# The turned edge order of a graph attention layer, worked out beside another layer's gathers

## The reference, cut to what matters

```python
def _L2_gnn_ref(x, edge_index, W, b):
    ...
    norm = dinv[src] * dinv[dst]
    xw = x @ W
    msgs = xw[src] * norm[:, None]
    agg = jax.ops.segment_sum(msgs, dst, num_segments=n)
    return jax.nn.relu(agg + b)

def _L3_gnn_ref(triplet_h, src, dst, Wqkv, bqkv, ...):
    h = layernorm(triplet_h, ln_attn_g, ln_attn_b)
    qkv = (h @ Wqkv + bqkv).reshape(n, 3, H, DH)
    ...
    scores = jnp.einsum('ehd,ehd->eh', q[src], k[dst])
    m = jax.ops.segment_max(scores, dst, num_segments=n)
    e = jnp.exp(scores - m[dst])
    sa = e / jax.ops.segment_sum(e, dst, num_segments=n)[dst]
    agg = jax.ops.segment_sum((v[src] * sa[:, :, None]).reshape(-1, D), dst, num_segments=n)
    ...
```

## Time and profile before

| | |
|---|---|
| median of 3 runs | 6839.76 us (6832.01 to 6848.44) |
| the profiled execution | 6829.43 us, span 6827.7 us |
| busy in the span | PE 45%, DVE 56%, ACT 26%, POOL 47% |
| DMA | 1056.28 MB, mean 155 GB/s |
| mean granted clock of TensorE | 0.713 of full speed |

### The profile page before, as it was taken

One profiled execution on the slowest core, in us unless ns is written; L12 is line 12 of the kernel. 1 busy time (PEld: TensorE's weight loads), 2 busy tenths in 40 slices (PEclk: granted clock), 3 DMA queues, 4 the chain that ended last, 5 costly groups with the idle time before them and its releaser, 6 DMA issues. The chain is left out here.

```text
span 6827.7 us, 78796 instructions
## 1 busy us (share of the span) xinstructions
PE 3084.9 (45%) x12973; PEld 1829.8 (27%) x12999; DVE 3813.8 (56%) x9383; ACT 1758.2 (26%) x4531; POOL 3197.0 (47%) x3216
## 2 busy tenths in 40 slices
PE   4467100345566666796001795001100157777638
PEld 3333100232243333343000342000100045555415
DVE  8998555467757776544334544344533546565551
ACT  1166000022226663111332211332100013232211
POOL 0000477667747773002776003776377625444430
PEclk9999555655567887898555897555555578888869
DMA  0000355456635553233665333665266428777630
GB/s 3 0 0 27 134 198 193 156 175 203 208 124 188 189 186 104 93 153 127 209 210 186 113 152 134 209 209 170 97 209 210 164 93 281 264 254 263 217 61 19
DMA packets 376599, 1056.28 MB, mean 155 GB/s; under 512 B 73682, under 2 KB 161140, under 8 KB 329876
## 3 DMA queue, kind: packets, MB, share of 16 engines
q1 hardware_dynamic: 211780, 588.53, 22.9%
q0 software_dynamic: 164688, 466.32, 22.6%
HBM read 537.47 MB, written 517.10 MB: 154 GB/s over the span
## 5 line engine op out<-in xcount | busy, mean ns | idle before, releaser
L940 POOL DMA_INDIRECT rows<-typed_table,index x832 | 813.1, 977 | 1183.1 <-DVE index L964 930.3
L940 POOL DMA_INDIRECT out_of<-table,index x936 | 968.4, 1035 | 464.9 <-issue 283.5
L979 DVE SCALAR_TENSOR_TENSOR state<-state,by_target_keep,rows 128x256 f32<-128x256 f32 x1248 | 604.8, 485 | 948.6 <-ACT rows L958 543.4
L940 POOL DMA_INDIRECT rows<-table,index x728 | 727.5, 999 | 317.8 <-issue 221.4
L1109 PE MATMUL bank<-ident,tail 128*128 128x128 f32 x6 | 2.0, 434 | 1658.8 <-PEq L74 1658.8
L2211 PE MATMUL bank<-weights,out_of 128*128 128x512 f32 x1600 | 698.3, 595 | 26.8 <-DVE weights L2259 26.8
L2603 POOL DMA_INDIRECT qv<-qv_table,index x416 | 410.6, 987 | 405.7 <-DVE index L2780 287.1
L979 DVE SCALAR_TENSOR_TENSOR y<-y,by_source_anew,out_of 128x256 f32<-128x256 f32 x897 | 435.4, 485 | 292.1 <-DMA out_of<-table,index 193.6
L958 ACT ACTIVATE rows<-rows,by_target_weight 128x256 f32<-128x256 f32 x832 | 343.0, 494 | 754.5 <-DMA rows<-typed_table,index 754.5
L1739 PE MATMUL bank<-x,marks 128*128 128x416 f16 x1664 | 392.8, 408 | 222.3 <-ACT marks L1753 222.3
L1109 PEld LDWEIGHTS bank<-ident,tail 128*128 128x128 f32 x6 | 0.9, 204 | 1659.9 <-issue 1659.9
(11 more groups left out here) (502 smaller groups left out, 6611.2 us busy)
## 6 DMA issues: line engine op xcount, KB each, us to landing
states<-state SPq DMA_DIRECT2D x195, 1024.0 KB, 4.3
states<-y SPq DMA_DIRECT2D x117, 1024.0 KB, 4.5
typed_table<-staged SPq DMA_DIRECT2D x400, 256.0 KB, 2.0
wide_states<-y SPq DMA_DIRECT2D x52, 1088.0 KB
near<-k_rows SPq DMA_DIRECT2D x416, 128.0 KB
out_of<-table,index POOLq DMA_INDIRECT x936, 2.9
rows<-typed_table,index POOLq DMA_INDIRECT x832, 2.9
rows<-table,index POOLq DMA_INDIRECT x728, 2.9
```

Of the source, the lines that this page charges most:

```text
L940: pool.indirect_dma_start(out=rows[h][:, u * D:(u + 1) * D], out_offset=None, in_=table, in_offset=bass.IndirectOffsetOnAxis(ap=index[h][: ...
L979: nc.vector.scalar_tensor_tensor(out=state[h][:, u * D:(u + 1) * D], in0=before, scalar=marks[:, bass.ds(g * GROUP + u, 1)], in1=rows[h][: ...
```

## The change

`StepOrder` becomes a companion. Its object is made at the start of the program, and `normalised_layer` hands it to the gather pass as `beside`, with `y` as the `spare` buffer. The phase of its own is gone. The DMAs are issued by ScalarE in place of SP; TensorE's part and VectorE's instructions are the same, VectorE's under `ahead`. `group` and `behind` are empty. Its ten semaphores are now among those of the pass (`step` and `cut` bear other names in the list).

```diff
-def normalised_layer(nc, env, order, x, out, own, w_dram, bias_dram, table, states):
+def normalised_layer(nc, env, order, x, out, own, w_dram, bias_dram, table, states, spare, steps):
...
-        edge_pass(nc, env, order, table, states, "sum", tail, [(bias[:], spread(bias_dram))], prepare=finish.prepare)
+        edge_pass(nc, env, order, table, states, "sum", tail, [(bias[:], spread(bias_dram))], prepare=finish.prepare, spare=spare, beside=steps)
...
 class StepOrder:
 
-    def __init__(self, stack, nc, by_source, by_target):
+    late = True
+    names = ("ready", "filed", "loaded0", "loaded1", "turned", "made", "marked", "summed", "settled", "kept")
+
+    def __init__(self, stack, nc, env, by_source, by_target, flat, window_table, k_rows):
...
-    def fill(self, nc, env, order, flat, window_table, k_rows):
...
-                @block.sync
-                def _(sp):
-                    sp.dma_start(flats[0].rearrange("(p t) -> p t", t=STEPS), order.keep[:]).then_inc(filed, 16)
...
+    def room(self, stack):
...
+        self.source_f, self.inner, self.total, self.quiet = (sb(n, STEPS) for n in ("source_f", "inner", "total", "quiet"))
...
+    def share(self, block, sems):
...
+        @block.scalar
+        def _(act):
+            nc.scalar.dma_start(flats[0].rearrange("(p t) -> p t", t=STEPS), order.keep[:]).then_inc(filed, 16)
+            act.wait_ge(ready, 1)
+            nc.scalar.dma_start(flats[1].rearrange("(p t) -> p t", t=STEPS), source_f[:]).then_inc(filed, 16)
+            act.wait_ge(filed, 32)
+            for a in range(2):
+                nc.scalar.dma_start(bulk(rows[a][:, 0:whole], MANY), flats[a][0:whole * P].rearrange("(k r q) -> r k q", k=MANY, r=P)
+                             ).then_inc(loaded[a], 16)
+                nc.scalar.dma_start(rows[a][0:rest, whole:whole + P], flats[a][whole * P:SLOTS].rearrange("(r q) -> r q", q=P)
+                             ).then_inc(loaded[a], 16)
+            act.wait_ge(ready, 2)
+            nc.scalar.dma_start(k_rows[ROWS:WINDOW_ROWS, :], zero[:]).then_inc(kept, 16)
+            act.wait_ge(settled, 1)
+            nc.scalar.dma_start(window_table.rearrange("u o -> o u"), self.window[0:1, :]).then_inc(kept, 16)
+            act.wait_ge(kept, 32)
...
+    def group(self, dve, g, h):
+        pass
+
+    def behind(self, dve):
+        pass
+
+    def ahead(self, dve):
...
+        then = counted_steps(dve, step)
+        nc.vector.tensor_copy(source_f[:], order.source[:]).then_inc(ready, 1)
+        nc.vector.memset(zero[:], 0.0).then_inc(ready, 1)
...
+        dve.wait_ge(turned, 1)
+        nc.vector.tensor_scalar(out=self.first[:], in0=env.bank[0][:, 0:STEPS], scalar1=-1.0, scalar2=1.0,
+                                op0=ALU.mult, op1=ALU.add).then_inc(cut, 1)
...
-            steps.fill(nc, env, order, flat, window_table, k_rows)
             row_norm(nc, x, y, gain[:], shift[:])
...
+        steps = StepOrder(stack, nc, env, by_source, by_target, flat, window_table, k_rows)
         x, y = buffer(stack, nc, "x", TILES * D), buffer(stack, nc, "y", TILES * D)
```

More of the change, by code:

```diff
@@ L2322 @@
 class StepOrder:
-    def __init__(self, stack, nc, by_source, by_target):
+    late = True
+    names = ("ready", "filed", "loaded0", "loaded1", "turned", "made", "marked", "summed", "settled", "kept")
+    def __init__(self, stack, nc, env, by_source, by_target, flat, window_table, k_rows):
+        self.nc, self.env, self.order = nc, env, by_target
+        self.flat, self.window_table, self.k_rows = flat, window_table, k_rows
         def sb(what, cols, dt=FP32):
@@ L2331, in __init__ @@
         self.place, self.chain_row = sb("place", TILES, I32), sb("chain_row", TILES, I32)
-    def fill(self, nc, env, order, flat, window_table, k_rows):
[L2336 to L2348, removed]
-                @block.sync
-                def _(sp):
-                    sp.dma_start(flats[0].rearrange("(p t) -> p t", t=STEPS), order.keep[:]).then_inc(filed, 16)
[L2353 to L2413, removed]
-                    then(nc.vector.tensor_tensor_scan(out=base[:], data0=env.ones[:, 0:TILES], data1=env.bank[7][:, 0:TILES], initial=0.0,
-                                                      op0=ALU.mult, op1=ALU.add))
-                    then(nc.vector.tensor_scalar(out=node[:], in0=env.iota_a1[:], scalar1=-1.0, scalar2=float(P), op0=ALU.add, op1=ALU.mult))
-                    then(nc.vector.tensor_scalar(out=node[:], in0=node[:], scalar1=env.own[:, 0:1], scalar2=base[:, TILES - 1:TILES],
-                                                 op0=ALU.add, op1=ALU.add))
-                    then(nc.vector.tensor_tensor(out=base[:], in0=base[:], in1=env.bank[7][:, 0:TILES], op=ALU.subtract))
-                    then(nc.vector.tensor_tensor(out=self.compact[:], in0=base[:], in1=env.bank[6][:, 0:TILES], op=ALU.add))
-                    then(nc.vector.tensor_tensor(out=node[:], in0=node[:], in1=self.compact[:], op=ALU.subtract))
-                    then(nc.vector.tensor_tensor(out=base[:], in0=self.compact[:], in1=node[:], op=ALU.subtract))
-                    then(nc.vector.tensor_tensor(out=base[:], in0=base[:], in1=order.some[:], op=ALU.mult))
-                    then(nc.vector.tensor_tensor(out=self.place[:], in0=base[:], in1=node[:], op=ALU.add))
-                    def step_of(out, edge):
-                        then(nc.vector.tensor_scalar(out=out[:], in0=edge[:], scalar1=0.5, scalar2=1.0 / P, op0=ALU.add, op1=ALU.mult))
-                        then(nc.vector.tensor_scalar(out=out[:], in0=out[:], scalar1=-0.5, scalar2=ROUND, op0=ALU.add, op1=ALU.add))
-                        then(nc.vector.tensor_scalar(out=out[:], in0=out[:], scalar1=-ROUND, scalar2=None, op0=ALU.add))
-                    step_of(base, order.start)
-                    then(nc.vector.tensor_copy(self.step_in[:], base[:]))
-                    then(nc.vector.tensor_tensor(out=last[:], in0=order.start[:], in1=order.count[:], op=ALU.add))
-                    then(nc.vector.tensor_scalar(out=last[:], in0=last[:], scalar1=-1.0, scalar2=0.0, op0=ALU.add, op1=ALU.max))
-                    step_of(step_out, last)
-                    then(nc.vector.tensor_tensor(out=last[:], in0=step_out[:], in1=base[:], op=ALU.is_gt))
-                    then(nc.vector.tensor_tensor(out=last[:], in0=last[:], in1=order.some[:], op=ALU.mult))
-                    then(nc.vector.scalar_tensor_tensor(out=step_out[:], in0=step_out[:], scalar=-float(STEPS), in1=last[:], op0=ALU.add, op1=ALU.mult))
-                    then(nc.vector.tensor_scalar(out=self.chain_row[:], in0=step_out[:], scalar1=float(STEPS), scalar2=None, op0=ALU.add))
-                    dve.wait_ge(summed, 2)
-                    then(nc.vector.tensor_copy(self.local[:], env.bank[2][:, 0:STEPS]))
-                    then(nc.vector.tensor_scalar(out=self.back_mark[:], in0=env.bank[5][:, 0:STEPS], scalar1=NEG, scalar2=None, op0=ALU.mult))
-                    then(nc.vector.memset(self.first[0:1, :], 1.0))
@@ new lines, in room, with sb @@
+    def room(self, stack):
+        def sb(name, cols, dt=FP32):
+            return buffer(stack, self.nc, name, cols, dt)
+        self.source_f, self.inner, self.total, self.quiet = (sb(n, STEPS) for n in ("source_f", "inner", "total", "quiet"))
+        self.rows = [sb("rows", (MANY + 1) * P) for _ in range(2)]
+        self.shifted, self.zero = sb("shifted", P + 1), sb("zero", D)
+        self.base, self.of_node, self.last, self.step_out = (sb(n, TILES) for n in ("base", "of_node", "last", "step_out"))
@@ new lines, in share, with _ @@
+    def share(self, block, sems):
+        nc, env, order = self.nc, self.env, self.order
+        self.sems = sems
+        ready, filed, loaded0, loaded1, turned, step, cut, summed, settled, kept = sems
+        loaded, rows, whole, rest = (loaded0, loaded1), self.rows, MANY * P, STEPS - MANY * P
+        inner, shifted, source_f, zero, k_rows, window_table = self.inner, self.shifted, self.source_f, self.zero, self.k_rows, self.window_table
+        flats = [self.flat[a * SLOTS:(a + 1) * SLOTS, :].rearrange("s o -> (s o)") for a in range(2)]
+        @block.scalar
[14 more added lines that the diff above has]
+            act.wait_ge(kept, 32)
+        @block.tensor
+        def _(pe):
+            for a in range(2):
+                pe.wait_ge(loaded[a], 32)
+                for k in range(MANY):
+                    nc.tensor.transpose(env.bank[a][:, k * P:(k + 1) * P], rows[a][:, k * P:(k + 1) * P], env.ident[:])
+                nc.tensor.transpose(env.bank[a][:, whole:STEPS], rows[a][0:rest, whole:whole + P], env.ident[0:rest, 0:rest]).then_inc(turned, 1)
+            pe.wait_ge(cut, 1)
+            nc.tensor.matmul(env.bank[3][:, 0:STEPS], env.ones[:], self.first[:], start=True, stop=True)
+            nc.tensor.matmul(env.bank[4][:, 0:STEPS], env.ones[0:1, :], self.first[0:1, :], start=True, stop=True)
```

(18 more changed lines are left out.)

52 lines of the change are left out of this document (added).

## The result

The changed kernel takes 6814.71 us (median of 9 runs, 6799.0 to 6828.71) against 6844.69 us before (9 runs, 6832.01 to 6848.44): ratio 0.9959, 95% interval 0.9947 to 0.9971. The forecast was 0.35% and 6816 us. Timed again in five rounds it was 0.9969 (0.9957 to 0.998). The medians are 30.0 us apart the first time and 24.1 the second, and the two profiled spans 6827.7 - 6803.0 = 24.7 us; so these measures of the gain lie between 24 and 30 us.

A forecast was written before the change was run, and what follows sets the result against it. No engine was busy over 56% of the span; POOL's gather chain was taken to set the pass's end. Terms -26.5 + 2.0 + 0.6 = -23.9 us, from 6839.8 to 6815.9 us (0.35% faster), range 6804 to 6833.

The forecast's parts named there:

- The sum: Whole kernel: -26.5 removed + 2.0 for slowed gathers + 0.6 for semaphores = -23.9 us.
- Removed, 26.5 us: Phase working out the turned edge order, between two barriers: cutting it saves 5507.83 - 5481.30 = 26.5 us.
- The ring covers the companion: Gather pass, third batch-normed layer: four loaded groups hide the companion's 25.0 us before fold group 0; cost nothing.
- my 5.6: Cover left in us: fifth group's index there at about 4915.7, POOL asking for it at 4921.3.
- Gathers slowed, 2.0 us: POOL's gathers beside the companion's VectorE work: 2.0 us added, from 0.2 per busy microsecond; bounds 0 and 13.5.
- Ten semaphores, 0.6 us: Phase closing the gather pass: ten more semaphores at 0.056 us each lengthen the barrier gap by 0.6 us.
- Lent buffers, nothing: Gather pass: three of four state buffers put into dead `y`; same instructions and bytes, so cost nothing.
- Rival 1: Gather pass: every busy VectorE microsecond delays POOL, 13.5 us; gain only 12.4, 6827.4 us; chance 0.06.
- Rival 2: Companion's DMA round trips: both 8 us longer would stall POOL 10.4 us, giving 6826.3 us; chance 0.07.
- Rival 3: Companion's store and four reads crawl at 11.95 us each, stalling POOL 43 us: 6859 us, slower; chance 0.03.
- Rival 4: Later attention stages absorb the earlier start, so the time comes back: 6840 us, the same; chance 0.06.
- the clock: TensorE's granted clock in the attention norm: 0.50 (1.2 GHz) with or without the removed phase; costed at nothing.

The follow-up runs named there:

- the repeat on a faster chip: Changed kernel timed again in five rounds with no edit, on a faster chip: 6810.03 us, ratio 0.9969 to the kernel before.
- the repeat there: Changed kernel run once more with no edit, on a slower chip: 7839.52 us, against 7865.95 for the kernel before.

## Why the prediction was right

The mechanism was as forecast: a serial phase went, and the ring hid what took its place. The sum came out near (-23.9 against -22.4 in the region, 24.7 in the spans), but in part by luck. What was removed is 27.4 us and not 26.5, and what was added 5.0 and not 2.6. Of the 5.0, 3.4 are in the gathers from first to last, 1.2 between the last gather and the next phase, 0.4 from there to the issue of the attention weights. That the time itself fell 1 us from the forecast is luck too, since the kernel before had 6844.69 us as its measure in place of the 6839.8 that I took.

- *Removed, 26.5 us:* right. From the issue of the attention weights to the norm it was 34.3 us and is 6.9, 27.4 less; 0.9 of that lie between the issue and the first instruction behind the next barrier, and why is open.
- *The ring covers the companion:* right. With the cover taken away, the same instructions behind the last fold bring the time back to that of before. The cover left was 6.8 us, and 6.8 again in the repeat on a faster chip; my 5.6 came from a companion of 28.6 us. It took 25.2 where it had taken 25.0 alone. The store and its read were 2.1 us apart under gathers, 1.5 less than alone, where I had 0.7 more; the reads and transposes were 1.2 slower, and VectorE lost 0.5 of the 1 us that I gave it.
- *Gathers slowed, 2.0 us:* mis-sized, and what I saw isn't the companion's. Gather 33 started 52.63 us after the first and before the change 52.26: 0.4 us. All of it is the third gather, 7.42 us and not 7.01, beside `prepare`, ahead of the companion; in the repeat on a faster chip it is 7.56 and gather 33 0.6 us later. The 20 gathers that start beside the companion are longer by 0.04 us together in the first profile, by 0.15 in that repeat, and by up to 0.7 on the slower chips. I took a rate per busy VectorE microsecond from a stretch of back-to-back operations on SBUF, and no run shows such a rate here.
- *Ten semaphores, 0.6 us:* right. The idle time in front of the next phase is 6.37 us with them, and 5.65 with lent buffers only: 0.7.
- *Lent buffers, nothing:* they cost perhaps 1 to 2 us that my sum didn't have.
- *Rival 1* (the gathers pay in full) fell with the 0.04 us. *Rival 2* (the round trips eat the cover) fell with the 2.1 us, on the slower chips too. Its stall did come in the repeat there, 5.23 us, but from VectorE's chained operations, which I had not among the rivals. *Rival 3* was a real mechanism with a wrong shape for this kernel: a store cut into 127 partitions and one takes 12.9 us, one of 128 doesn't. *Rival 4* fell: the stages behind the norm took 1319.9 us and take 1321.8. The norm's stretch is at the granted clock 0.50 after the change as before, so the clock cost nothing there.

## What to carry to other kernels

A phase that is a chain of small steps costs its whole length; moved into the idle start of a ring it costs nothing as long as chain plus first fold is shorter than the ring's loaded depth. Here 6.8 us were to spare in both profiles on faster chips and none in the one on a slower chip. So compute that slack first, from the time at which the ring's producer asks for its first slot again. Next to a software gather cut long VectorE operations on SBUF into pieces and put them where VectorE waits: one of 6.8 us held one gather for as long. Keep plain transfers at 128 partitions when something waits for them.

## What the runs showed of the hardware

Three things I hadn't expected. A dependent store and read on ScalarE's queue under gathers were 2.1 us apart, and on SP's with no gathers beside them 3.6. The queue isn't the reason: behind the last fold, with no gathers, they were 4.0 us apart on ScalarE's queue (5407.35 and 5411.37). In both slow cases another store had been issued within 0.5 us ahead, in the fast one none; that this is the cause isn't shown. Eight short VectorE operations that read PSUM left the gathers beside them at 0.95 us, while one 128x6400 operation with two SBUF inputs held a gather for its whole 6.8 us. And chips differ by 16% on this program (6838 against 7917 us before), with the same durations of single instructions but up to 1.4 us between starts in VectorE's chained small operations and over 2 us between chained folds, so that a cover measured on one chip is not a cover on another.
